# Second attention of a hybrid transformer block on one core: shifted scores nine units behind the scores, two units of scores before the last key selection, the bias addition behind the low parts, and a reordered end

## What is computed

```python
qkv = x @ qkv_w.T + qkv_b            # 16 heads of 8
q = q * cos + _rotate_half(q) * sin  # k likewise
attn = softmax(einsum('abhqd,abhkd->abhqk', q, k) * scale)
out = einsum('abhqk,bhkd->abhqd', attn, v) ... @ proj_w.T + proj_b
# second FFN: normalised x, logits = x @ router_w.T, sigmoid, best 4 of 8 groups,
# best 8 of 64 experts, gated experts weighed by them, plus a shared expert
```

## Time and profile before

| | |
|---|---|
| median of three runs | 1091.7 us (1087.84 to 1092.44) |
| profiled execution, its own time | 1089.98 us |
| its span | 1088.2 us |
| TensorE / VectorE / ScalarE / GpSimd busy | 90% / 89% / 62% / 34% |
| granted TensorE clock, mean | 0.868 |
| chain that ended last | TensorE 39%, VectorE 3% of the span |

### The profile page before, as it was taken

How to read it: one execution, slowest core, us unless ns; L and a number is a source line. 1 busy time by engine, 2 the same in 40 slices (tenths; PEclk the granted TensorE clock), 3 DMA queues, 4 the chain that set the end, 5 groups by cost and what they waited for, 6 DMA issues and landing times. The chain is left out here.

```text
span 1088.2 us, 17668 instructions
## 1 busy us (share of the span) xinstructions
PE 980.7 (90%) x5408; PEld 706.8 (65%) x5408; DVE 965.0 (89%) x1448; ACT 675.5 (62%) x855; POOL 374.6 (34%) x300
## 2 busy tenths in 40 slices
PE   6867888777669999999999889999989999999997
PEld 4633444444347888888888546555668888888885
DVE  7689999999988999999999788888789999999996
ACT  4679999999934454454454556776544454454553
POOL 2044666667901343343341131111113343343330
PEclk9765555555659999999999999999989999999999
DMA  2000000000108656555550000111149555555521
GB/s 59 1 1 1 1 1 1 1 1 1 52 20 206 174 147 154 156 141 160 151 147 15 1 1 1 23 24 20 26 98 235 157 146 157 154 142 161 150 72 39
DMA packets 50711, 86.94 MB, mean 80 GB/s; under 512 B 20092, under 2 KB 33404, under 8 KB 50556
## 3 DMA queue, kind: packets, MB, share of 16 engines
q1 hardware_dynamic: 50664, 86.34, 30.8%
HBM read 83.33 MB, written 2.98 MB: 79 GB/s over the span
## 5 line engine op out<-in xcount | busy, mean ns | idle before, releaser
L1535 ACT ACTIVATE sg<-ps 128x512 f32<-128x512 f32 x264 | 156.8, 594 | 265.4 <-PE ps L539 264.6
L539 PE MATMUL ps<-xh,whi 128*128 128x512 f32 x528 | 206.7, 391 | 1.3 <-ACT b L1357 1.3
L539 PE MATMUL ps<-xh,wlo 128*128 128x512 f32 x528 | 206.1, 390 | 0.0
L539 PE MATMUL ps<-xl,whi 128*128 128x512 f32 x528 | 206.0, 390 | 0.0
L2064 DVE TENSOR_TENSOR hf<-sg,ps 128x512 f32<-128x512 f32 x264 | 170.7, 684 | 30.5 <-DVE hl L2383 24.3
L1755 POOL CAST whi<-wraw 128x384 fp32r<-128x384 f32 x66 | 66.8, 1012 | 365.3 <-PE ps L539 285.4
L1675 POOL TENSOR_TENSOR rr<-xr,rr 128x2048 f32<-128x2048 f32 x32 | 145.3, 4577 | 126.8 <-ACT rr L1332 71.1
L2383 DVE TENSOR_TENSOR hl<-hf,hh 128x1024 fp32r<-128x1024 f32 x132 | 178.1, 1349 | 0.5 <-DVE hf L2064 0.5
L2388 DVE TENSOR_TENSOR hf<-hf,cbc 128x1024 f32<-128x1024 f32 x128 | 157.6, 1231 | 13.4
L1541 ACT ACTIVATE hh<-hf 128x1024 fp32r<-128x1024 f32 x132 | 139.1, 1054 | 4.6 <-DVE hf L2388 4.6
L1757 POOL TENSOR_TENSOR wlo<-wraw,whi 128x384 fp32r<-128x384 f32 x66 | 115.3, 1747 | 5.3
(11 more groups left out here) (276 smaller groups left out, 1543.6 us busy)
## 6 DMA issues: line engine op xcount, KB each, us to landing
cbc<-routing_coefficients SPq DMA_DIRECT2D x256, 256.0 KB, 3.8
wraw<-in_wexp_dram SPq DMA_DIRECT2D x66, 192.0 KB, 2.8
X<-in_x_dram SPq DMA_DIRECT2D x4, 256.0 KB, 4.8
routing_coefficients<-cT SPq DMA_DIRECT2D x8, 128.0 KB, 2.3
out_dram<-X SPq DMA_DIRECT2D x4, 256.0 KB, 2.9
heads_by_row<-o_all SPq DMA_DIRECT2D x12, 72.0 KB
b_rows<-heads_by_row SPq DMA_DIRECT2D x12, 72.0 KB, 2.7
rope_in<-in_consts_dram SPq DMA_DIRECT2D x1, 512.0 KB, 3.4
```

What stands on the lines that cost most here:

```text
L539: return pe.matmul(o, l, r, start=start, stop=stop, **kw)
L1535: act.activation(sg[c % 2][:, :], bank(4 + 2 * (c % 2)), ACT.Silu).then_inc(s_sg, 1)
```

## The change

In the loop the shifted scores follow nine units behind the scores, where they followed eight. Every step of the path that is keyed to V stays at its V; ScalarE's steps of the path, keyed to U, are set one U earlier, so that they meet the same V. The loop without shifted scores again has six slots (V = 3 to 8, formerly 2 to 7), because the scores of units 1 and 2 are now issued one head at a time (`b_score_head`) around the last q selection. The tail has one more slot of shifted scores. GpSimd's addition of the bias waits for the low parts of all four groups. SP loads each of the four pieces once that piece is stored, instead of after all four. ScalarE takes the rounding `f_high` out of `copy_xT` and does it two or three units later. In the tail TensorE's steps stand at one U less, VectorE divides the third quarter's rows before the sigmoids, and 12 matmuls instead of 6 fill the place ahead of the last transposition.

```diff
-AHEAD = QUAD + 4
+AHEAD = QUAD + 5
...
-        s_ost = sem("b_heads_stored")
+        s_ost = [sem(f"b_heads_stored{j}") for j in range(4)]
...
                 for j in range(4):
-                    sp.dma_start(o_d[c, j, :, :], o_all[32 * j:32 * j + VH, c, :]).then_inc(s_ost, 16)
-                sp.wait_ge(s_ost, 64 * (c + 1))
+                    sp.dma_start(o_d[c, j, :, :], o_all[32 * j:32 * j + VH, c, :]).then_inc(s_ost[j], 16)
                 if c >= 1:
                     sp.wait_ge(s_on, B + c)
                 for j in range(4):
+                    sp.wait_ge(s_ost[j], 16 * (c + 1))
                     sp.dma_start(b_rows[:, j, :, :], o_d[c, j, :, :].rearrange("x (p r) -> p x r", r=16)
                                  ).then_inc(s_old, 16)
...
                         b_tiles(-1, 0)
-                        keep_busy(2, 8)
+                        keep_busy(3, 8)
+                        b_score_head(1, 0)
                     select_q_b(g)
                     if g + 1 < GROUPS:
                         values_b(g + 1)
                     else:
-                        keep_busy(2, 3)
-                        b_tiles(-1, 1)
+                        b_score_head(1, 1)
+                        b_score_head(2, 0)
+                        b_score_head(2, 1)
...
-            TAIL_FILL = {56: 1, 57: 1, 58: 2, 59: 2, 60: 2, 61: 1, 62: 2, 63: 1, 64: 3}
+            TAIL_FILL = {55: 1, 56: 1, 57: 1, 58: 2, 59: 2, 60: 2, 61: 1, 62: 2, 63: 1, 64: 3}
...
+            def b_score_head(V, i):
+
+                if 2 * V + i >= 3:
+                    pe.wait_ge(s_mx, 2 * V + i - 2)
+                for half in range(MT):
+                    last = b_score_step(V, half, i)
+                last.then_inc(s_s1, 1)
...
-                for V in range(2, AHEAD):
+                for V in range(3, AHEAD):
...
-                    elif U == 56:
+                    elif U == 55:
                         pe.wait_ge(s_mx, 2 * B * UNITS - 1)
                         logits(1, 0, 0)
...
-                if U == 57:
+                if U == 56:
                     pe.wait_ge(s_mx, 2 * B * UNITS)
                     logits(1, 0, 1)
-                elif U == 60:
+                elif U == 59:
                     pe.wait_ge(s_q2, 2 * B)
                     pe.wait_ge(s_on, B + 3)
                     transposed(2, 7)
                 elif U == 61:
                     pe.wait_ge(s_sc, lap(1, 0, 1))
-                elif U == 62:
                     projected(2, 1)
...
-                keep_busy(4, 6)
+                keep_busy(4, 12)
...
+                    if U == 56:
+                        logit_exps(1, 0, (0,))
                     if U < B * UNITS:
...
-                    if U == 57:
-                        logit_exps(1, 0, (0,))
...
-                    if U in (27, 43):
-                        o_transposed_b((U - 27) // 16, 7)
-                    elif U in (34, 50):
-                        f_norm_rstd(1, (U - 34) // 16)
-                    elif U in (52, 56):
-                        copy_xT((U - 52) // 4, 7)
-                    elif U == 58:
+                    if U in (26, 42):
+                        o_transposed_b((U - 26) // 16, 7)
+                    elif U in (33, 49):
+                        f_norm_rstd(1, (U - 33) // 16)
+                    elif U in (51, 55):
+                        copy_xT((U - 51) // 4, 7)
+                    elif U in (53, 58):
+                        act.wait_ge(s_fxT, GROUPS + 1 + (U - 53) // 5)
+                        f_high((U - 53) // 5)
+                    elif U == 57:
                         logit_exps(1, 0, (1,))
-                    elif U == 61:
+                    elif U == 60:
                         o_transposed_b(2, 7)
...
                 act.activation(f_xT[g][:, :], bank(n), ACT.Copy).then_inc(s_fxT, 1)
-                act.wait_ge(s_fxT, GROUPS + g + 1)
-                f_high(g)
...
                 copy_xT(2, 7)
+                act.wait_ge(s_fxT, GROUPS + 3)
+                f_high(2)
...
                 pool.wait_ge(s_xn, 2 * GROUPS)
+                pool.wait_ge(s_lo, 2 * GROUPS)
                 pool.tensor_tensor(xb, xb, pb_s[:, :].unsqueeze(1).broadcast_to([P, TILES, P]), ALU.add
...
                 x_low(1, 0, 0)
                 marks(1)
+                normalise(2)
                 sigmoids(1, 0, 0)
+                shift(2 * B - 1)
                 x_low(1, 0, 1)
-                shift(2 * B - 1)
-                normalise(2)
                 sigmoids(1, 0, 1)
```

## The result

| | before | changed |
|---|---|---|
| median of 4 runs each, side by side | 1089.77 us (1087.82 to 1092.44) | 1071.38 us (1069.85 to 1078.80) |
| ratio, 95% interval | | 0.9847 (0.9800 to 0.9894) |
| profiled execution, its span | 1089.98 us, 1088.2 us | 1078.80 us, 1077.0 us |
| TensorE / VectorE / ScalarE / GpSimd busy | 90 / 89 / 62 / 34% | 90 / 89 / 63 / 35% |

The changed kernel is faster by 1.5%. The same program ran again in two later comparisons, with ratios of 0.9893 (0.9861 to 0.9925) and 0.9888 (0.9848 to 0.9928), medians 1074.91 and 1075.18. The profiled execution is the slowest of its four; where it would mislead I read the repeated run `e4_after_again` beside it.

What follows compares the result with a forecast made beforehand. It took TensorE and VectorE as both near their limit, their order deciding. Terms -4.6 + 0.15 - 0.3 + 1.4 - 0.25 = -3.6 us gave 1086.4 from the profile, 1088.1 from the median; forecast 1087.2, range 1083 to 1091.5.

Steps and rivals of the forecast that it cites:

- Loop: Whole loop: plain periods rise from 6.25 to 6.41 us, periods with fills or other work partly offset it; +0.15 us.
- The wait for bank 6: In the loop, ahead of the PV behind the copy of bank 6: grows from 0.15 to about 0.6 us.
- Rival 1: Loop falls to VectorE's floor, bank 6 copied earlier, periods reach 5.85 us; sum -7.3, total 1083; chance 0.15.
- Start: Preparation's end: later bias addition and earlier single heads' scores let V = 3 issue 4.7 us earlier; -4.6 us net.
- Bias addition: Preparation's end: GpSimd's addition, moved beside the maxima, costs nothing there; at most 2.84 us if it blocked VectorE.
- Rival 2: Preparation's end: bias addition still blocks VectorE, returning 2.84 us; sum -0.8, total 1090; chance 0.08.
- ScalarE's rounding: Rounding among exponentials at V = 60 and 64 moves to free ScalarE time; bounds 0 and 0.63, taken as -0.3 us.
- Turns: Turns by memory (V = 34, 35 and 50, 51): later copy balanced by piecewise loads, 0; otherwise up to 1.4 us each.
- Rival 3: Turn by memory is late: two turns of 1.2 us; sum -1.2, total 1089.6; chance 0.10.
- Tail: Tail: one more slot of 1.67 us, one fill fewer elsewhere gives back 0.25; +1.4 us.
- End: End: six more fills hold the clock; half of VectorE's 0.47 us wait is saved; -0.25 us.
- Rival 4: Loop: TensorE's longer waits make the clock fall, 1.4 us each; five falls give +3.4, total 1093.4; chance 0.07.

Runs made afterwards that it cites:

- e4: The changed kernel run again unchanged, for a second profile (`e4_after_again`): 1074.91 us, ratio 0.9893 to the kernel before.
- e3: Kernel before, with only GpSimd's bias addition waiting for the low parts of all groups: 1081.68 us, ratio 0.9951.
- e1: Kernel before, lag eight, with row groups swapped in every second group of eight units, so V and V - 8 differ: 1081.69 us, ratio 0.9935.
- e9: Changed kernel's other main parts and e8's fills, but lag eight with e1's row-group swap and the rounding still in the copy: 1072.92 us, ratio 0.9862 to the kernel before.
- e10: e9 with ScalarE's rounding later (U = 54 and 59) and the last shift ahead of the second low part: 1073.73 us, ratio 0.9867 to the kernel before.
- e2: Changed kernel, lag nine, with e1's swap, so V and V - 9 share row groups in seven slots of eight: 1085.24 us, ratio 0.9966 to the kernel before.
- e8: Changed kernel with three more filling matmuls behind the single heads' scores, ahead of the last k selection: 1074.14 us, ratio 0.9863 to the kernel before.
- e6: Changed kernel with SP issuing the loads only after all four stores have landed, as before: 1076.89 us, ratio 0.9893 to the kernel before.
- e7: Changed kernel with six filling matmuls instead of twelve ahead of the last transposition: 1075.89 us, ratio 0.9896 to the kernel before.

## Why the prediction was wrong, step by step

- **Loop, forecast +0.15, measured about -10.8** (B to C fell by 9.34 with the tail's +1.4 inside). This step failed. It carried the 0.67 us of a slot's tiles over from the earlier trace rows as if it were a property of eight matmuls. It was one of eight matmuls on two row groups, and the lag of nine made it 0.45. Most of the miss is here. The stretch from B to the last transposition of the maxima, taken from one trace to the next, splits the 10.8: 1.5 to the clock, which in the kernel before fell at the first turn and in e3 did not; 7.0 to the row groups (e3 to e1); 0.6 to ScalarE's later rounding (e9 to e10), which has a term of its own below; 1.6 to the lag of nine itself (e10 to the changed kernel). The sign named beforehand, plain periods of 6.2 or less, came.
- The wait for bank 6 grew, as said, but to 0.21 and not 0.6, since the exponentials ahead of the copy get their scores earlier: the PV starts 2.34 after the slot of the copy (689.22 - 686.88), not 2.55. With the row groups shared (e2) the forecast's 6.41 and 2.54 came out.
- A TensorE saving of four times 0.22 a period would be 0.9. Plain periods gained 0.52, since the 5.74 lie only a little above VectorE's 5.4. Periods in which TensorE has other work, and VectorE therefore room, mostly gained 0.8 to 1.1 (7.96 became 6.85, 7.77 became 6.72), of which 0.3 to 0.5 is the lag's own.
- **Rival 1** was nearest to the outcome, a loop close to VectorE's limit, with a total of 1083. It gave the wrong mechanism (an earlier copy), and its floor of 5.85 a period was none: the changed kernel takes 5.74 and e1 5.66. The prediction had 0.65 for a maximum from a row of six in the earlier trace rows, which holds two short pauses; they start 0.60 apart where nothing holds them up.
- **Start, forecast -4.6.** The sum came out where the clock held, -4.8 at V = 5 in e8 and e9, but partly by luck. The forecast was 2.84 for the bias addition and 1.9 for the scores ahead, less a little. e3, with the late addition alone and a full clock, is already 4.05 earlier: 2.85 for the wait, as forecast, and 1.2 for a fall of the clock that the kernel before had around 648 and that I had not priced. The scores ahead bring the rest, 0.8 at V = 5 and 1.2 at V = 9 (e9), about half of their term. In the changed kernel's own executions the clock fell during the selections, and from A to B -1.3 was left in e4, and +1.4 in the first profile. I had not weighed a fall of the clock here, though fills and short waits alternate in it as at the turn in the earlier trace rows.
- **Bias addition.** Right. The Trainium skill, page "SBUF — State Buffer", section "Who interferes with whom", was cited for `tensor_reduce` being free of the block; by that rule, the trace agrees, with 0.68 to 0.69 us for each of the four maxima, which read PSUM, beside the addition. Rival 2 is refuted.
- **ScalarE's rounding, forecast -0.3.** Measured -0.63 at lag eight (e10 against e9), the upper of my two bounds.
- **Turns, forecast 0.** The division follows the shift without a wait, and the first turn took 8.31 against 8.83 undisturbed, from the shorter tiles. With the loads together it would have waited 0.94 (e6): the loads by pieces do what I had set against the later copy. Rival 3 is refuted for these two turns. The third division, moved ahead of the sigmoids, does come too early for its loads:

```profile
754.15 0.56 DVE L2301 RECIPROCAL b_rden<-b_rows 128x64 f32<-128x64 f32 x1 [3.50 <-DMA b_rows<-heads_by_row]
```

  VectorE's new order was said not to be late. In the changed kernel this wait costs TensorE nothing, but in e6, where it is 4.62, it reaches TensorE.
- **Tail, forecast +1.4.** From the last transposition of the maxima to C: 15.25 before, 16.67 in seven of the eight profiles with the lag of nine (17.13 in e6), +1.42. Right.
- **End, forecast -0.25, measured -1.2.** Too small. The last logits in the changed kernel, and the sum on VectorE, which waited 0.47 in the earlier trace rows:

```profile
784.03 0.66 ACT L1527 ACTIVATE sc<-ps 128x256 f32<-128x256 f32 x2 [0.53 <-PE ps L539]
785.04 0.68 DVE L1951 TENSOR_TENSOR sfc<-sc,eb_s 128x512 f32<-128x512 f32 x1
```

  The wait of 0.47 is gone. C to D takes 29.53 before, 29.04 in e9, 28.58 in e10 and 28.37 in the changed kernel. So half a us comes with the earlier division and the fills, and another half with the later rounding and the earlier last shift, which I had costed at nothing there; the last 0.2 is not taken apart. Six fills do as well as twelve (e7). The clock, on which I had rested this term, is not what it hangs on: it still fell to 0.50 in the changed kernel at 784, and before and e3 both take 29.53 though it was low for 10 us in the one and for 7 in the other.
- **Rival 4**, a clock that falls in the loop: not behind B in the changed kernel's three profiles, where B to C is the same to 0.03 us. A fall of the clock did strike at the preparation's end.

## What to carry to other kernels

When TensorE works on slices of 32 rows, ask of every pair of matmuls that stand next to each other on which rows they lie. A change of distance in a software pipeline changes that silently, and an unchanged list of instructions can take two thirds of its time. A duration taken from a row holds for the neighbours that it had there, and a mean taken from a merged row may hold pauses.

A gain measured at one place is worth what the next engine leaves of it (here 0.5 of 0.9 us a period), and a gain beside a stretch where TensorE waits may be lost to its clock: compare the stretches, not only the totals.

## What was not expected of the hardware

- Four matmuls of 32 rows by 256 columns on four row groups start within 0.02 us and finish together; eight take 0.45 us to the next instruction, against 0.67 when two groups are shared by pairs. The Trainium skill, page "TensorE: Matmul & The Clock Gate", section "The mechanism" of part 3, says that weight loads overlap running matmuls only if the row groups differ, and that tiles on different groups then run side by side. The trace agrees: in the shared order the third matmul starts 0.22 us after the first, in the other order it starts with it.
- The clock between A and B differed between executions of one program: 0.74 and 0.87 from 640 to 648 in two profiles of the changed kernel. Ahead of the fills TensorE had waited 0.55 us in the one and 0.54 in the other. In the first the clock fell among the fills, at 640.5, in the second only during the last selection of k, at 646.0. In e3 and e9 the same wait of 0.55 was followed by no fall. The difference stays unexplained.
- VectorE's maxima (128x512, from PSUM) take 0.68 to 0.69 us each and start 0.60 apart back to back, before, in e1 and in the changed kernel alike. The page's rows give 0.61 to 0.65 for a mean, which differs only by the pauses in them.
